# The end of the retention stage laid over the first steps of local attention, without a barrier between them

## Time and profile before

| | |
|---|---|
| median of 3 runs | 1138.23 us (1133.57 to 1142.29) |
| the profiled execution | 1135.86 us, its span 1134.1 us |
| PE busy | 889.7 us, 78% of the span |
| DVE busy | 670.4 us, 59% |
| ACT busy | 491.2 us, 43% |
| POOL busy | 451.6 us, 40% |
| mean granted PE clock | 0.885 |

### The profile page before, as it was taken

One profiled execution on the slowest core, in us unless ns is written; L12 is line 12 of the kernel. 1 busy time (PEld: TensorE's weight loads), 2 busy tenths in 40 slices (PEclk: granted clock), 3 DMA queues, 4 the chain that ended last, 5 costly groups with the idle time before them and its releaser, 6 DMA issues.

```text
span 1134.1 us, 19013 instructions
## 1 busy us (share of the span) xinstructions
PE 889.7 (78%) x6776; PEld 539.6 (48%) x6776; DVE 670.4 (59%) x1760; ACT 491.2 (43%) x1010; POOL 451.6 (40%) x461
## 2 busy tenths in 40 slices
PE   6864898889755887899578648978898468879993
PEld 3542576457533444444335425764675334444442
DVE  5874795669575764320358747956794856643103
ACT  4111675377424563631041127753774245635310
POOL 3453783288250422200135538832882304222001
PEclk9885999999987797899878869999999777978997
DMA  9000110011000000000100001100110000000001
GB/s 362 21 1 10 25 30 6 13 31 26 1 1 1 1 1 1 1 1 0 38 3 1 1 10 25 34 1 19 25 25 2 0 1 1 1 1 1 1 1 37
DMA packets 11630, 21.62 MB, mean 19 GB/s; under 512 B 1424, under 2 KB 6928, under 8 KB 11024
## 3 DMA queue, kind: packets, MB, share of 16 engines
q1 hardware_dynamic: 11248, 18.60, 5.6%
q10 hardware_dynamic: 288, 1.78, 0.4%
HBM read 11.87 MB, written 1.05 MB: 11 GB/s over the span
## 4 chain that ended last, share of the span: by engine, by line
PE 49%; DVE 24%; POOL 11%; issue 9%; ACT 4%; DMA 1%; POOLq 1%; SPq 0%; DVEq 0%; ACTq 0%
PE bank L794 10%; PE bank L369 9%; PE bank L715 4%; DVE arena L1173 4%; PE bank L490 3%; PE bank L784 2%; DVE arena L1034 2%; DVE arena L859 2%; POOL arena L1608 2%; POOL arena L1621 2%; POOL arena L1629 2%; PE bank L612 2%; PE bank L701 2%; PE bank L682 2%; POOL arena L1634 2%
## 5 line engine op out<-in xcount | busy, mean ns | idle before, releaser
L1303 ACT ACTIVATE arena<-bank 128x512 f32<-128x512 f32 (+2 forms) x300 | 146.1, 557 | 182.4 <-PE bank L369 122.7
L369 PE MATMUL bank<-consts_sb,arena 128*128 128x128 f32 x1024 | 160.7, 300 | 78.6 <-DVE arena L1165 26.2
L369 PEld LDWEIGHTS bank<-consts_sb,arena 128*128 128x128 f32 x1024 | 125.2, 153 | 150.4 <-issue 81.0
L1580 POOL TENSOR_TENSOR rstd<-vareps,neghalf 128x1 f32<-128x1 f32 x96 | 54.1, 564 | 252.6 <-DVE vareps L854 251.0
L1173 DVE TENSOR_REDUCE arena<-bank 128x2 f32<-128x1024 f32 (+3 forms) x128 | 98.1, 818 | 80.7 <-PE bank L669 80.1
L1677 POOL TENSOR_SCALAR_AFFINE_SELECT arena<-arena 128x256 f32<-128x256 f32 x128 | 51.1, 412 | 201.6 <-ACT arena L1491 198.9
L1621 POOL TENSOR_TENSOR arena<-arena,neghalf 128x16 f32<-128x16 f32 x32 | 92.9, 2904 | 85.0 <-DVE arena L1036 84.7
L490 PE MATMUL bank<-weights,x_features 128*128 128x512 f32 x192 | 103.6, 665 | 13.5 <-DVE arena L1049 8.0
L794 PE MATMUL bank<-arena,weights 128*128 128x512 f32 x256 | 111.9, 594 | 1.6 <-ACT arena L1547 1.6
L1491 ACT ACTIVATE arena<-bank 128x1024 f32<-128x1024 f32 (+1 forms) x96 | 81.5, 881 | 36.9 <-PE bank L701 36.8
L1418 ACT ACTIVATE arena<-bank,arena 128x128 f32<-128x128 f32 x256 | 69.5, 383 | 49.7 <-DVE arena L1075 49.7
(11 more groups left out here) (167 smaller groups left out, 1633.4 us busy)
## 6 DMA issues: line engine op xcount, KB each, us to landing
arena<-arena SPq DMA_DIRECT2D x56, 130.0 KB, 2.3
weights<-wts_dram SPq DMA_DIRECT2D x1, 2824.0 KB, 19.3
weights<-wts_dram SPq DMA_DIRECT2D x1, 1817.0 KB, 13.4
weights<-wts_dram SPq DMA_DIRECT2D x1, 1561.0 KB, 9.5
x_tokens<-x_dram SPq DMA_DIRECT2D x6, 256.0 KB, 3.2
consts_sb<-consts_dram ACTq DMA_DIRECT2D x1, 1226.5 KB, 7.1
out_dram<-x_inner SPq DMA_DIRECT2D x16, 64.0 KB, 1.6
consts_sb<-consts_dram SPq DMA_DIRECT2D x1, 768.0 KB, 4.7
```

Of the source, the lines that this page charges most:

```text
L369: mm = pe.transpose(bank[:, i * P:(i + 1) * P], src, ident)
L1303: return act.activation(dst, src, ACT.Copy)
```

## The change

- The barrier is gone. Retention's pipeline ends at step 8 on every engine, and what is left of it stands inside the first steps of local attention: on DVE `residual(5)` to `residual(7)` and the layer norms of tiles 4 to 7 at the head of steps 0 to 3, and `gated(7)` behind the rotation of step 0; on PE and ACT `gathered(6)` and `gathered(7)` (and on PE their projections) in steps 0 and 1; on POOL the `root` of tiles 5 to 7 in steps 0 to 2.
- In a retention step of DVE `gated(s-2)` is now the last piece, behind `normalise(s-1)`.
- `tables` is done by POOL, ahead of its retention loop.
- The blanking (`pads`) is done by POOL before its last retention tile, once `outputs(7)` is done; PE waits for it and for the tables at the first scores of local attention, ACT no longer waits for it.
- `window_features(1)` of the first layer moves from step 0 to step 3.
- The slices of `arena` are laid out anew, so that what the first steps of local attention write is dead by then in retention.

```diff
-        def retention_end(eng):
-            eng.drain().then_inc(retention_done, 1)
-            eng.wait_ge(retention_done, 4)
+        SECOND_AT = (3, 0)
...
 # PE, retention (gathered and project_heads are the same code, moved out)
-                for s in range(1, G + 3):
+                for s in range(1, G + 1):
                     if s < G:
                         scores(s)
                     if s >= 3:
                         gathered(s - 3)
-                    if s <= G:
-                        outputs(s - 1)
+                    outputs(s - 1)
                     if s >= 3:
-                        project(s - 3)
-                    if s <= G:
-                        back(s - 1)
+                        project_heads(s - 3)
+                    back(s - 1)
 # PE, window_layer
                         project(n, 1, "k", pe_k, (swapped_ready, 2 * n + 2))
+                        if n < 2:
+                            gathered(G - 2 + n)
...
                         project(n, 2, "v", pe_v, (vA_ready, n + 1))
-                        if g == 0:
+                        if n < 2:
+                            project_heads(G - 2 + n)
+                        if g == SECOND_AT[l]:
                             window_features(1)
...
+                        if n == 0:
+                            pe.wait_ge(tables_ready, 1)
+                            pe.wait_ge(pads_ready, 1)
 # DVE, retention
-                for s in range(1, G + 5):
-                    if s == 6:
-                        tables()
+                for s in range(1, G + 1):
                     if s < G:
                         masked(s)
-                    if 2 <= s <= G + 1:
+                    if s >= 4:
+                        residual(s - 4)
+                    if s >= 5:
+                        retention_normed(s - 5)
+                    if (s - 1) % NT < NT - 1:
+                        update_state(s - 1)
+                    normalise(s - 1)
+                    if s >= 2:
                         gated(s - 2)
-                    ...
 # DVE, window_layer
+                        if n < 3:
+                            residual(G - 3 + n)
+                        if n < 4:
+                            retention_normed(G - 4 + n)
                         dve.wait_ge(sq_ready, 2 * n + 2)
...
+                        if n == 0:
+                            gated(G - 1)
                         if g in FIRST_TILES:
 # ACT, window_layer
+                        if n < 2:
+                            gathered(G - 2 + n)
                         act.wait_ge(pe_v, n + 1)
...
-                        if g == 0:
+                        if g == SECOND_AT[l]:
                             window_features(1)
 # POOL, retention
-                for s in range(G + 4):
+                tables()
+                for s in range(G):
                     g = s
+                    if g == G - 1:
+                        pads()
...
+            def pads():
+                pool.wait_ge(pe_o1, G)
+                pool.memset(kk2[:, 0, :, 0:64], 0.0)
+                pool.memset(vS2[:], 0.0)
+                pool.drain().then_inc(settle, 1)
+                pool.memset(vS2[:, :, :, D2:D2 + 1], 1.0)
+                pool.memset(vA2[:, :, :, D2:D2 + 1], 1.0)
+                pool.drain().then_inc(pads_ready, 1)
 # POOL, window_layer
+                    if l == 0 and s < 3:
+                        root(LN1 + G - 3 + s)
```

More of the change, by code:

```diff
@@ L95, in build @@
         neg3 = sb("negmax3", [P, 16], F32R)
-        ARENA = 22600
-        STAGING = 22400
+        ARENA = 23000
+        STAGING = 22800
         arena = sb("arena", [P, ARENA])
@@ L119, in build @@
         VW = H1 * (V1 + 1)
[L120 to L123, removed]
+        a1 = carve([("v", G * 512), ("scaled", 4 * S), ("qx", 4 * S), ("PT", 2 * 2048), ("qT", 2 * S), ("kT", 2 * S),
+                    ("kM", 2 * S), ("state", 2 * 512), ("gap", 64), ("gate", G * 256), ("small2", 344),
+                    ("statetmp", VW), ("on", 512), ("sq", 256), ("cg", 512), ("y", 512), ("yT", 512), ("oE", 1024),
+                    ("z", 256), ("den", 16), ("ss", 16), ("gvar", 32), ("grstd", 32)])
         qT1 = a1["qT"].rearrange("p (b s) -> p b s", b=2)
@@ L214, in counter @@
             return s
-        retention_done = counter("retention_done")
         x_next = counter("x_next")
@@ L376, in features, with gathered, project_heads @@
                 transposes(bank, [xM[:, 4 * b + t, :] for t in range(NT)]).then_inc(pe_xT, 1)
+            def gathered(g):
+                pe.wait_ge(y_ready, g + 1)
+                bank = take(pe, ("yT", g), [(yT_ready, g + 1)], bank=BANK1["yT"])
+                transposes(bank, [y1[:, g % 2, 0:P], y1[:, g % 2, P:2 * P]]).then_inc(pe_yT, 1)
+            def project_heads(g):
+                pe.wait_ge(loaded[1], 16)
+                bank = take(pe, ("wo1", g), [(z1_ready, g + 1)], bank=BANK1["wo1"])
+                pe.wait_ge(yT_ready, g + 1)
+                for k in range(2):
+                    mm = pe.matmul(bank[:, 0:P], yT1[:, g % 2, k * P:(k + 1) * P],
+                                   w_("wo1")[:, k * P:(k + 1) * P], start=(k == 0), stop=(k == 1))
+                mm.then_inc(pe_wo1, 1)
             def retention():
@@ L438, in back @@
                     transposes(bank, [oE1[:, g % 2, r * P:(r + 1) * P] for r in range(4)]).then_inc(pe_back, 1)
[L440 to L452, removed]
                 for b in range(2):
@@ L860, in norm_apply, with gated, residual, retention_normed @@
                                          ALU.subtract, ALU.mult)
+            def gated(g):
+                dve.wait_ge(grstd_ready, g + 1)
+                dve.wait_ge(cg_ready, g + 1)
+                if g >= 2:
+                    dve.wait_ge(pe_yT, g - 1)
+                dve.tensor_tensor(y1[:, g % 2, :].rearrange("p (h d) -> p h d", h=H1), cg1[:, g % 2],
+                                  grstd1[:, g % 2, :].unsqueeze(2).to_broadcast([P, H1, V1]), ALU.mult)\
+                    .then_inc(y_ready, 1)
+            def residual(g):
+                dve.wait_ge(pe_wo1, g + 1)
+                dve.wait_ge(xb1_ready, 1)
+                if g >= 2:
+                    dve.wait_ge(xM_ready, g - 1)
+                dve.tensor_tensor(z1[:, g % 2, :], held(("wo1", g))[:, 0:P], xi[:, g, :], ALU.add)\
+                    .then_inc(z1_ready, 1)
+                dve.wait_ge(z1_ready, g + 1)
+                norm_stats(LN1 + g, [z1[:, g % 2, :]])
+            def retention_normed(g):
+                norm_apply(LN1 + g, xM[:, g, :], z1[:, g % 2, :]).then_inc(xM_ready, 1)
             def retention():
@@ L933, in normalise @@
                         .then_inc(gvar_ready, 1)
[L935 to L952, removed]
                 projected(0)
@@ L958, in retention @@
                 values_gates(1)
-                for s in range(1, G + 5):
-                    if s == 6:
-                        tables()
+                for s in range(1, G + 1):
                     if s < G:
                         masked(s)
-                    if 2 <= s <= G + 1:
-                        gated(s - 2)
[L966 to L991, removed]
+                    if s >= 4:
[6 more added lines that the diff above has]
+                    if s >= 2:
+                        gated(s - 2)
             def gated_hidden(l, b, kb):
@@ L1289, in _ @@
                 retention()
-                retention_end(dve)
                 for l in range(2):
@@ L1307, in features, with gathered @@
                 evac(hT[:, b, 1:S + 1], held(("xT", c))[:]).then_inc(xT_ready, 1)
+            def gathered(g):
+                act.wait_ge(pe_yT, g + 1)
+                if g >= 2:
+                    act.wait_ge(pe_wo1, g - 1)
+                evac(yT1[:, g % 2, :], held(("yT", g))[:, 0:256]).then_inc(yT_ready, 1)
             def retention():
@@ L1335, in retention @@
                 key_tokens(1)
-                for s in range(1, G + 3):
+                for s in range(1, G + 1):
                     if s >= 3:
[L1338 to L1348, removed]
+                        gathered(s - 3)
+                    g = s - 1
+                    act.wait_ge(pe_o1, g + 1)
+                    if g >= 2:
+                        act.wait_ge(pe_back, g - 1)
+                    evac(oE1[:, g % 2, :], held(("oT1", g))[:]).then_inc(oE_ready, 1)
             def window_layer(l):
@@ L1581, in root, with tables @@
                     .then_inc(rstd_ready, 1)
+            def tables():
+                pool.wait_ge(consts_loaded[2], 16)
+                pool.wait_ge(rows_loaded[1], 16)
+                for dst, name in ((band_bf[:, 0, :], "band_first"), (band_bf[:, 1, :], "band"),
+                                  (ident_bf[:], "ident")):
+                    pool.tensor_copy(dst, c_(name))
+                first, last = ROWS["g3"][0], ROWS["b3"][0] + 256
```

(8 more changed lines are left out.)

15 lines of the change are left out of this document (1 added, 14 removed).

## The result

The changed kernel took 1100.51 us in the median, against 1135.91 us for the kernel before in runs beside it: ratio 0.967, 95% interval 0.9616 to 0.9725. The forecast was 1101, the range 1088 to 1118. One of its four executions took 2766 us, for a reason that is not known: the ratio leaves it out, the median counts it, and the median of the other three is 1099.03. The profiled execution took 1102.0 us around a span of 1100.2.

What follows compares the result with a forecast made beforehand. It took the serial chain between retention and local attention, and DVE in steps 1 to 7, as the bound. Gains of 21.3 less 3.5 us, 17.8 a pass, 35.6 for two, gave 1100.3, stated as 1101 us; range 1088 to 1118.

Steps and rivals of the forecast that it cites:

- tables and waits: Retention steps 1 to 7: 3.5 us a pass from tables moved to POOL, 3.0 net from the gate at the step's end.
- the seam: From retention's step 8 to local attention's first sum of squares: one serial chain, shortened by 14.8 us a pass.
- local attention's first steps, B less A: Cost 3.5 us a pass; A: `masked(1)` to first sum of squares, B: `masked(1)` to sum of tile 4.
- Tables: DVE's step 6 loses 3.5 us to tables; on POOL they fit idle time at cost 0: gain 3.5 us a pass.
- Gate: DVE's step end: waits of 3.1 and 1.45 us go, 1.6 us of new ones come, net gain 3.0 us a pass.
- The hold of L859 by the memsets: Norm of tile 3 ends with POOL's blanking, at 5.6 us after step 8's head instead of 3.7.
- The features' chain and POOL's chain: Before the first sum: PE's features end 12.6 us after step 8's head, POOL's power and root allow 11.9; 12.5 taken.
- T + 14: Late bound for the first sum, 14 us after DVE reaches step 8's head, if half clock already holds in step 8.
- The serial loop of the slower rival: Retention steps: PE and DVE take turns at half clock, 10.5 us a step, 6.3 us a pass lost, 1149 us; chance 0.04.
- The last step of the sum: Two passes' gain taken off the profiled 1135.9 us gave 1100.3; lying 2.4 us below the median, it became 1101.

Runs made afterwards that it cites:

- blank last: The changed kernel with the blanking as the last piece of POOL's retention loop, behind the last power and root: 1094.93 us, ratio 0.9607.
- root first: The changed kernel with POOL's root of tile s-3 ahead of the gate product and power of tile s: 1097.57 us, ratio 0.9623.
- gate before norm: The changed kernel with DVE's gate between the state update and the head normalisation of the same step: 1092.51 us, ratio 0.9599.
- the blanking behind the inverse norms: The changed kernel with root early, gate ahead of head normalisation, and blanking behind POOL's first inverse norms of local attention: 1081.16 us, ratio 0.9493.
- gate in old place: The changed kernel with DVE's gate back behind the masks, as before the change: 1106.47 us, ratio 0.972.
- root first and blank last: The changed kernel with POOL's root ahead of gate product and power, and the blanking last in its retention loop: 1097.73 us, ratio 0.9633.

## Why the prediction was right

The sum held term by term. For the first pass, with the rows above (the second gave 6.1, 14.6 and -3.6):

| term | forecast | measured |
|---|---|---|
| tables and waits, from masks to the variance before step 8 | 3.5 + 3.0 = 6.5 | 51.8 - 45.4 = 6.4 |
| the seam, from there to the first sum | 14.8 | 27.3 - 12.8 = 14.5 |
| local attention's first steps, B less A | -3.5 | 33.6 - 35.8 = -2.2; second pass -3.6 |

**Tables.** Right: 7.7 us on POOL in its idle time, and 3.6 to 3.9 us a pass back when undone.

**Gate.** The net was right and its parts were not. I put 0.7 us of new wait on step 3; it was 2.0, since I took full clock there and PE ran at half after its pause: its transposes and outputs took 1.4 us longer than they do at full clock. Step 4 had 0.55 for 0.7. The 0.31 us of `normalise` waiting for PE in step 6 went too, which I had not counted. That the gate's move gives something is shown (A is 2.4 and 3.0 us longer when it is undone); that the step's end is its best place is not so.

**Seam.** The hold of L859 by the memsets, the coupled guess of the sum, came as written: 2.08 us, ending with the memset. The features' chain and POOL's chain ended 1 us apart, as forecast. But this is how only the first pass goes. In the second the half clock of the last outputs did the same, for the same price. The sum had the hold with full clock in both passes and no half clock in step 8 short of its bound of T + 14; that the second pass agrees as well (14.6) is luck. The two cover one another, as the run with the blanking last shows.

**Local attention.** 2.2 and 3.6 us against 3.5. The serial loop of the slower rival was seen in step 3, and with 0.55 us in step 4: PE held by L867, and DVE idle; in steps 5 to 7 DVE had no wait.

**What is left.** B got 18.7 and 17.2 us shorter, 35.9 in all, but the span only 33.9. The other 2.0 are spread over stages in which the code did not change: up to the second pass they were 2.4 us shorter, behind it 4.3 longer. The largest is in the second pass, where the same sixteen transposes, after the same pause of 1.69 us, took 3.67 us for 1.97, at a granted clock of 0.50 for 1.00. The kernel before, then the changed one:

```profile
744.00 1.97 PE L369 MATMUL bank<-consts_sb,arena 128*128 128x128 f32 x16 [1.69 <-POOL arena L1634]
```

```profile
705.77 3.67 PE L368 MATMUL bank<-consts_sb,arena 128*128 128x128 f32 x16 [1.69 <-POOL arena L1654]
```

So a time within 2 us of the forecast is partly luck: 1.3 us that local attention took less than forecast in one pass stood against 2 us elsewhere. The last step of the sum was also loose: 1100.3 was to be the profiled execution, and with the 2.4 us that this lay below the median the forecast would have been 1102.7, not 1101.

## What to carry to other kernels

Where every engine is thin between two stages, follow the one chain that crosses the barrier and lay the second stage's head beside the first one's tail; then look at what each queue now does in the middle of the seam, since an instruction with no hurry (a blanking, a power) is what the urgent one waits behind. A piece moved to relieve one engine belongs behind the moment its input is ready and no later: the gate at the step's end cured DVE's wait and made PE's. Waits can cover each other: a hold that went gave 2.3 us in one pass and nothing in the other, where the engine behind it was late too, so an edit is judged by the waits in the trace as well as by the time. Over the whole kernel the parts nearly added up: by the ratios blank last, root first and gate before norm gave 0.6, 0.5 and 0.7%, and the three together, with the blanking behind the inverse norms, 1.8%.

## What the runs showed of the hardware

- A TENSOR_SCALAR of DVE from SBUF to SBUF did not end beside a POOL memset. L859 took 2.08, 2.07 and 1.32 us for 0.35 (changed, blank last, gate in old place) and ended within 0.1 us of the memset's end each time.
- Not every POOL instruction does this. Beside POOL's power of 128x16 (74.89 to 77.92 us in root first) L859 took its 0.34 us.
- What is queued behind a held instruction shows the hold in its own busy time (L942 1.52, a TENSOR_REDUCE 1.81), but it need not lose that time. With root first and blank last, three TENSOR_TENSORs stood behind a held one of 0.17 us; all four ended at 89.65, and the next started at 89.21, as long behind the first as without a memset (1.3 us):

```profile
87.87 1.78 DVE L1022 TENSOR_SCALAR arena<-arena 128x16 f32<-128x16 f32 x1
87.95 1.70 DVE L1031 TENSOR_TENSOR arena<-bank,rotary 128x512 f32<-128x512 f32 x1
88.55 1.10 DVE L1033 TENSOR_TENSOR arena<-bank,rotary 128x256 f32<-128x256 f32 x1
88.88 0.77 DVE L1035 TENSOR_TENSOR arena<-bank,rotary 128x256 f32<-128x256 f32 x1
89.21 0.68 DVE L1031 TENSOR_TENSOR arena<-bank,rotary 128x512 f32<-128x512 f32 x1
```

- A TENSOR_SCALAR from PSUM ran beside a memset at its full pace: 0.17 us at 626.75, with POOL's memset of 128x2080 from 625.24 to 627.07. TENSOR_TENSORs that did not stand behind a held instruction did so too (1.22 and 1.29 us in the kernel with the blanking behind the norms).
- The same pause does not always bring the same clock: after 3.19 us PE's outputs of the last tile ran at a granted clock of 1.00 in the first pass, after 3.18 at 0.50 in the second.
- POOL's power of 128x16 took 3.00 to 3.05 us in the changed kernel's retention from the second on, where DVE's gate starts beside it, and 2.89 to 2.93 with the gate in its old place or before the normalisation.
